# Reordering the gate, up and down weight loads on one DMA queue of a transformer layer

## What is computed

```
x = x + layernorm(attention(layernorm(x)))     # 16 heads of 64, block-sparse, blocks of 64
x = x + layernorm(ffn(layernorm(x)))

gate = x @ w_gate.T ; up = x @ w_up.T          # 1024 -> 3072, weights int32 / 127
ffn  = (silu(gate) * up) @ w_down.T            # 3072 -> 1024
```

## Time and profile before

| | us |
|---|---|
| median of 3 runs | 2469.5 |
| lowest run | 2467.34 |
| the profiled execution | 2468.2 |
| its span, slowest core (core 2) | 2466.7 |
| spans of the 8 cores | 2447.7 to 2466.7 |
| span of `_p3a` on core 2, about | 909 to 1554 |
| span of `_p4` on core 2, about | 1554 to 2466.7 |

### The profile page before, as it was taken

How to read it: one execution, slowest core, us unless ns; L and a number is a source line. 1 busy time by engine, 2 the same in 40 slices (tenths; PEclk the granted TensorE clock), 3 DMA queues, 4 the chain that set the end, 5 groups by cost and what they waited for, 6 DMA issues and landing times.

```text
span 2466.7 us, 31915 instructions; the slowest of 8 cores (2447.7 to 2466.7 us)
## 1 busy us (share of the span) xinstructions
PE 1663.9 (67%) x11110; PEld 806.2 (33%) x11234; DVE 863.8 (35%) x2468; ACT 602.3 (24%) x807; POOL 340.8 (14%) x512
## 2 busy tenths in 40 slices
PE   0079999977776730103654266389898998989896
PEld 0034444444454420001221022134343443434342
DVE  3413343434443443344344333332223222222323
ACT  2411111166546611012221222211111111111111
POOL 1012212111121120000110011012120212111120
PEclk9999999966677665556787688699999999999998
DMA  9923232311221048437875475367584857476572
GB/s 228 269 82 85 69 76 78 103 53 54 87 67 57 19 86 131 112 102 125 140 121 126 111 107 77 128 86 86 87 84 90 76 96 77 79 93 90 73 82 85
DMA packets 361579, 239.36 MB, mean 97 GB/s; under 512 B 313040, under 2 KB 318800, under 8 KB 359376
## 3 DMA queue, kind: packets, MB, share of 16 engines
q0 software_dynamic: 227536, 111.33, 32.5%
q1 hardware_dynamic: 120064, 92.43, 14.7%
q10 hardware_dynamic: 13824, 33.56, 3.9%
HBM read 205.53 MB, written 75.63 MB: 114 GB/s over the span
## 4 chain that ended last, share of the span: by engine, by line
PE 37%; DVE 11%; DMA 5%; ACT 3%; issue 3%; SPq 2%; ACTq 1%; DVEq 0%; POOL 0%; POOLq 0%
PE gp L245 13%; PE upp L250 13%; PE yp L277 6%; DMA p_ctx<-ctxT_d 3%; PE upp L277 3%; PE gp L277 3%; DVE p_attn L854 2%; DVE p_attn L852 2%; DVE p_x L892 2%; ACT p_x L950 2%; ACT p_xn L971 1%; SPq L316 1%; DVE bst3b L899 1%; DVE bst L859 1%; DVE bst3b L901 1%
## 5 line engine op out<-in xcount | busy, mean ns | idle before, releaser
L245 PE MATMUL gp<-x2T,wg_sb 128*128 128x512 bf16 x1504 | 382.7, 397 | 435.7 <-DVE hswb L208 195.7
L250 PE MATMUL upp<-x2T,wu_sl 128*128 128x512 bf16 x1507 | 365.1, 383 | 1.5
L245 PEld LDWEIGHTS gp<-x2T,wg_sb 128*128 128x128 bf16 x1536 | 153.8, 101 | 631.4 <-issue 463.9
L208 DVE TENSOR_TENSOR hswb<-hswb,upp 128x256 bf16<-128x256 bf16 x384 | 144.0, 418 | 586.2 <-PE upp L250 530.3
L291 POOL DMA_DIRECT2D wu_sl<-wuT x192 | 168.2, 878 | 1032.1 <-PE upp L250 1013.7
L687 ACT ACTIVATE arenaB<-pp 128x768 bf16<-128x768 f32 (+2 forms) x312 | 232.2, 1084 | 148.2 <-PE pp L644 148.2
L277 PE MATMUL yp<-wd_sb,hswb 128*128 128x512 bf16 x846 | 190.5, 384 | 83.6 <-DVE y_sb L223 74.2
L198 ACT ACTIVATE hswb<-gp 128x512 bf16<-128x512 f32 x192 | 114.0, 597 | 501.9 <-PE gp L245 501.7
L250 PEld LDWEIGHTS upp<-x2T,wu_sl 128*128 128x128 bf16 x1536 | 152.5, 99 | 188.8 <-issue 13.8
L644 PE MATMUL pp<-qt_buf,kt_buf 64*64 64x64 bf16 (+2 forms) x3232 | 155.8, 309 | 77.0 <-ACT arenaB L687 64.3
L524 PE MATMUL qp<-xn1T,wq_sb 128*128 128x512 bf16 x490 | 121.5, 383 | 122.9 <-DMA xn1T<-xn_d 121.6
(11 more groups left out here) (85 smaller groups left out, 1295.7 us busy)
## 6 DMA issues: line engine op xcount, KB each, us to landing
wu_sl<-wuT POOLq DMA_DIRECT2D x192, 256.0 KB, 4.8
xbuf<-x_in SPq DMA_DIRECT2D x32, 512.0 KB, 11.1
p_x<-x_in SPq DMA_DIRECT2D x32, 512.0 KB, 5.0
x_d<-p_x ACTq DMA_DIRECT2D x32, 512.0 KB, 6.4
x1f<-x_d SPq DMA_DIRECT2D x32, 512.0 KB, 4.5
out<-obuf POOLq DMA_DIRECT2D x32, 512.0 KB, 5.4
ctxT_d<-cstage POOLq DMA_DIRECT2D x128, 65.0 KB, 2.0
xn_d<-xn1buf ACTq DMA_DIRECT2D x32, 256.0 KB, 7.2
```

The source lines that it names most:

```text
L208: v.tensor_tensor(hold["hswb"][:, hc * 512 + o:hc * 512 + o + 256], hold["hswb"][:, hc * 512 + o:hc * 512 + o + 256], hold["upp"][:, (ghc ...
L245: mm = te.matmul(gsl, hold["wg_sb"][:, dc * FF + hc * 128:dc * FF + (hc + 1) * 128], xsl(dc), start=(dc == 0), stop=(dc == 7))
L250: mm = te.matmul(usl, hold["wu_sl"][:, (hc % 3) * 1024 + dc * 128: (hc % 3) * 1024 + (dc + 1) * 128], xsl(dc), start=(dc == 0), stop=(dc = ...
```

## The change

Only the order of GpSimd's queue in `_p3a` changes; the same loads are issued with the same waits. Before: the four gate quarters, up blocks 0 to 7, down quarter 0, up 8 to 15, down quarter 1, up 16 to 23, down quarters 2 and 3, up of chunk 1. After: up 0 to 2, gate quarter 0, up 3 to 8, gate quarter 1, up 9 to 14, gate quarter 2, up 15 to 20, gate quarter 3, up 21 to 23, down quarters 0 to 3, up of chunk 1.

```diff
-                for qq in range(4):
+                def wg_q(qq):
                     srcw = wgT_d[:, qq * (FF // 4):(qq + 1) * (FF // 4)]
                     dst = hold["wg_sb"][:].rearrange("p (dc c) -> p dc c", dc=8)[
                         :, :, qq * (FF // 4):(qq + 1) * (FF // 4)]
                     g.dma_start(dst,
                                 srcw.rearrange("(dc p) c -> p dc c", p=128)).then_inc(s_wg_t[qq], 16)
-                wu_loads(g, 0, 0, 8)
-                for qr in range(4):
+
+                def wd_q(qr):
                     srcw = wdT_d[qr * 768:(qr + 1) * 768, :]
                     g.dma_start(
                         hold["wd_sb"][:, qr * 6 * DM:(qr + 1) * 6 * DM].rearrange(
                             "p (hc c) -> p hc c", hc=6),
                         srcw.rearrange("(hc p) c -> p hc c", p=128)).then_inc(s_wd_t[qr], 16)
-                    if qr == 0:
-                        wu_loads(g, 0, 8, 16)
-                    elif qr == 1:
-                        wu_loads(g, 0, 16, 24)
+                wu_loads(g, 0, 0, 3)
+                wg_q(0)
+                wu_loads(g, 0, 3, 9)
+                wg_q(1)
+                wu_loads(g, 0, 9, 15)
+                wg_q(2)
+                wu_loads(g, 0, 15, 21)
+                wg_q(3)
+                wu_loads(g, 0, 21, 24)
+                for qr in range(4):
+                    wd_q(qr)
                 wu_loads(g, 1, 0, 24)
```

## The result

| | before | after |
|---|---|---|
| median of the runs (42 each) | 2472.53 us | 2482.35 us |
| ratio of after to before | | 1.0029, 95% interval 1.0015 to 1.0043 |
| the profiled execution, spans of its cores | 2447.7 to 2466.7 us | 2454.0 to 2471.2 us |

The change makes the kernel slower, by 0.29% or about 7 us, where 11 us faster was forecast; 2482 lies outside the range of 2447 to 2473. The medians include runs in which the cores of one die were granted a lower clock; the ratio leaves those out.

A forecast was written before the change was run, and what follows sets the result against it. The norm stream was taken to bound `_p3a`, with `_p4` held fixed. Terms -12.9 - 2.0 - 2.0 - 2.0 + 8 = -10.9 took the profiled 2468.2 to 2457.3, so a median of 2458 us; range 2447 to 2473.

The forecast's parts named there:

- What bounds the kernel: In `_p3a` the norm stream is critical, not TensorE; its changes pass to the total one for one, `_p4` fixed.
- Part 1: Start of `_p3a`: with three gate quarters gone, iteration 2's transposes take 13.3 us instead of 26.2; gain 12.9 us.
- Part 2: Iterations 7 to 9: gate quarters 1 to 3 land just in time; gain 2.0 us in each iteration.
- cover of blocks 6 and 7: Iteration 7: the stall moves ahead of block 6, under norm work; both blocks end before VectorE takes block 6's product.
- everything is ready: Iteration 7: blocks 6 and 7 are done before the product and block 8 are due, by 4 and 1.8 us.
- clock gain: Blocks 8 and 14: TensorE, no longer idle before them, runs gate matmuls at the higher clock, saving 2.0 us each.
- rival of late quarters: Blocks 6, 12, 18: gate quarters landing after 26.4 us cost 6 us each, total 2482 us; chance 0.13.
- harmless burst: Iteration 10: the four down quarters cost the transposes nothing; sum -18.9, total 2450 us; chance 0.11.
- no gain at the start: Iteration 2's transposes were slow because of input loads; sum +2, total 2471 us; chance 0.04.
- Part 3: Down quarters' burst: transposes before iteration 11 run at half speed until 1320 us; loss 8 us, bounds 0 and 18.
- rival in which the burst takes back what the start gave: Transposes before iteration 11 make no headway until 1320 us; loss 18 us, total 2468 us; chance 0.14.
- The sum: Whole kernel: -12.9 - 2.0 - 2.0 - 2.0 + 8 = -10.9 us, giving 2458 us.

The follow-up runs named there:

- e1: Kernel before with all four down quarters moved behind up block 23, gate quarters left alone; ratio 1.0076, 19 us slower.
- e5: As e2, but gate quarters 1 to 3 issued two up loads earlier, behind up blocks 6, 12 and 18; ratio 0.9924 to the kernel before.
- e7: Kernel before, with x1 and xn2 writes in six iterations issued only once the next iteration's p_ctx transposes have landed; ratio 0.9902.
- e2: Changed kernel, but down quarters issued one each after the p_ctx transposes of iterations 2 to 5; ratio 0.9963 to the kernel before.
- e3: Kernel before, but gate quarter 0 behind up block 2, quarters 1 to 3 after the p_ctx transposes of iterations 2, 3, 4; ratio 0.9936.
- e4: As e3, but down quarters spread too: after the transposes of iterations 5 and 6, behind up blocks 10 and 16; ratio 0.9933 to the kernel before.
- e9: Kernel before with three down quarters behind up block 23 instead of two; ratio 1.0042, iteration 10 8.5 us longer.

## Why the prediction was wrong

**What bounds the kernel** was read rightly. TensorE's stall did move ahead of blocks 6, 12 and 18, `_p4` did not change, and the norm stream set the length of `_p3a`: each term passed through to the total, to within 3 us (e1 to e5).

**Part 1, the start: right mechanism, wrong size.** -12.9 was forecast and called nearly all there is to have; -18.5 came. The failing step is the choice of iteration 3 as the undisturbed case. Its 13.3 us already held 5 us of the writes of x1 and xn2, which iteration 2 does not have. After shows 7.8 and 13.2 us side by side, and e7 shows that the writes are the cause: 8.3 us once they are moved. Iteration 4 of the kernel before, 8.0 us, would have given the right price ahead of the run.

**Part 2, the gate quarters just in time: wrong sign, -6.0 forecast, +6.5 measured.** The landing was somewhat early (11.2 to 15.2 us over the cores against 16.6), and the cover of blocks 6 and 7 held. The step that failed is "everything is ready": it counted blocks 6 to 8 and not what is issued once block 6 is done. The up load of block 9 moves behind the pause into the p_ctx transposes, lands after 16.0 us instead of being there long before, and holds TensorE up to 4.4 us on core 7, at a point without cover. e2 has this loss without the burst, e3 and e4 have the gate quarters early and don't have it, and e5 removes it by 7 us of lead. The clock gain of three times 2 us, the other half of this term, failed as well: on core 7 3.2 to 3.8 us of idling and then the wait for the next block's up load lie in the way, and e5 got nothing from it either. The rival of late quarters had this side right, for the wrong reason; the quarters weren't late. The rivals of a harmless burst and of no gain at the start fell with e1 and e3.

**Part 3, the burst: right mechanism, half the size, +8 forecast, +16.8 measured.** The rival in which the burst takes back what the start gave held the price at 18 us. The forecast let the transposes run at half speed, but ended the burst at 1320 us as if it ran alone. The transposes slow the burst just as well. On core 7 of after the last p_ctx transpose (1321.5) and the last up load (1320.7) end within 1 us of each other, 33 us after the x2T issue. Counted so, with both sides sharing, the chain loses as much time as the queue still has work when x2T is issued, at most its own 15 us: four quarters (the first after 15.4 us, the others 9 us apart) and three up loads (a sixth of a quarter's bytes, so 1.5 us each) are 47 us of work from the first issue, of which 30 have passed at the x2T issue, so 16 to 17 remain, more than the chain's own 15; in e9 about 7 remain; before, none (the last up load lands before x2T is issued on core 0, 1289.8 against 1291.3). That gives 15, 7 and 0 where 16.8 to 18.4, 8.5 and 0 were measured, 2 to 3 us too little for the burst of four. This estimate was made after e9, and no run tested it by itself.

**The rule of the Trainium skill** in its page "DMA: Bandwidth & Descriptors", section "Anatomy of one DMA — SWDGE (gpsimd) path" (an estimate of 5.6 us for a quarter), does not hold here: the gate quarters of the rows above took 14.2 us and more, and the shortest landing of a quarter in any profiled execution is 10.6 us (core 0 of e5, a down quarter). The same page of the Trainium skill says in "Queues, rings and completion order" that an engine takes turns between its queues, packet by packet. The mutual slowing of burst and transposes agrees with that, and the forecast would have come nearer had it been applied to both sides.

**The sum.** -18.5 + 6.5 + 16.8 = +4.8 us; the profiled pair has +2.5 in `_p3a`, and the runs say +7. Against the forecast these are 5.6 us more gain at the start, 12.5 us more loss in iterations 7 to 9 and 8.8 us more in iteration 10, and they do not cancel. The forecast's own addition had a slip besides. Its 8 us of part 3 are counted from an x2T issue that is already 2 us earlier, and the sum takes these 2 us of iteration 9 off once more; by its own figures the sum is -8.9 us, about 2460 us (and 2457.3 + 1.3 is 2458.6). Neither changes which steps failed.

What stays open: steps whose transposes run beside writes differ by up to 2.5 us each between executions of kernels that are alike there (steps 4 to 6 take 61.3 us before and 57.7 in e9, in whose queues nothing differs by then); no run explains it.

## What to carry to other kernels

A load that is delayed until just before its use also delays everything that waits for that use, so follow the next loads behind the pause and ask which transfers they now meet. Before taking another iteration as the undisturbed price of a step, list every queue that issues beside it: here the writes on ScalarE's queue hid 5 us per iteration, and moving them was worth as much (1.0%) as the best reordering of the weights (0.8%). A bulk load belongs in the window between one landing and the next issue on the critical queue, one piece at a time; a wait on that landing's semaphore puts it there.

## What the runs showed of the hardware

- A 1.5 MB piece from GpSimd's queue, converted from int32 to bf16, lands 11 to 18 us after its issue when it is alone or the first of several (the down quarters of before, after, e2 and e5), and pieces behind each other come 8 to 11 us apart; in the gate load at the start of before they come 9 to 14 us apart.
- A p_ctx step of two transposes and an input load takes 7.8 to 8.3 us by itself, 13.3 beside 1.5 MB of writes from ScalarE's queue, and 26.2 beside a bulk load on GpSimd's queue, on the cores shown; over all cores of before and after it is 6.8 to 8.6 (iteration 4 of before, 2 of after), 11.1 to 14.5 (iteration 3) and 24.4 to 28.0 (iteration 2 of before).
- Four x2T transposes that SyncE issues in 7.05 us beside the writes alone, and in 4.9 to 5.0 us with the writes moved (e7), took 14.0 to 19.2 us to issue beside the burst of four (after and e1, all cores): the issue itself is held up, and with it what stands behind it in SyncE's queue.
